# Second cross attention of a perceiver block: queries once, then turned to context space

## The reference, cut to what matters

```
q = layernorm(x) @ Wq            # 256 -> 16 heads x 128
k, v = ctx @ Wk, ctx @ Wv        # 128 -> 16 heads x 128
q = q * rsqrt(mean(q*q) + eps) * gq
k = k * rsqrt(mean(k*k) + eps) * gk
x = x + softmax(q @ k.T * scale) @ v @ Wo
```

## Time and profile before

| | |
|---|---|
| median of the runs | 2654.81 us |
| the profiled execution's own time | 2667.95 us |
| its span, from first to last instruction | 2666.0 us |
| busy, share of the span | PE 95%, PEld 71%, DVE 51%, ACT 48%, POOL 29% |
| mean granted TensorE clock | 0.983 |
| bridge | about 1203 to 1269 us |
| second cross attention | about 1270 to 1930 us |
| DMA, mean | 73 GB/s |

### The profile page before, as it was taken

One profiled execution on the slowest core, in us unless ns is written; L12 is line 12 of the kernel. 1 busy time (PEld: TensorE's weight loads), 2 busy tenths in 40 slices (PEclk: granted clock), 3 DMA queues, 4 the chain that ended last, 5 costly groups with the idle time before them and its releaser, 6 DMA issues. The chain is left out here.

```text
span 2666.0 us, 56230 instructions
## 1 busy us (share of the span) xinstructions
PE 2538.4 (95%) x16582; PEld 1904.6 (71%) x16582; DVE 1350.9 (51%) x4801; ACT 1269.6 (48%) x5190; POOL 769.3 (29%) x979
## 2 busy tenths in 40 slices
PE   7999999999999999998899999999879999999888
PEld 6888888878544444445677777777768888888777
DVE  3555555546677754446434455444424444444434
ACT  2555555544466666665545665556412222222142
POOL 1332232347355520003424323231061111111132
PEclk9999999999899999999999999999989999999999
DMA  6222222110510024422534543333380000000033
GB/s 191 71 63 65 66 64 66 53 46 0 167 48 2 1 72 134 128 58 62 145 103 125 138 111 93 85 100 89 107 205 5 8 8 8 5 7 8 8 92 122
DMA packets 176273, 195.16 MB, mean 73 GB/s; under 512 B 39993, under 2 KB 141687, under 8 KB 175378
## 3 DMA queue, kind: packets, MB, share of 16 engines
q1 hardware_dynamic: 146146, 157.65, 20.6%
q0 software_dynamic: 17744, 32.60, 5.3%
q10 hardware_dynamic: 12256, 3.44, 0.8%
HBM read 150.44 MB, written 56.62 MB: 78 GB/s over the span
## 5 line engine op out<-in xcount | busy, mean ns | idle before, releaser
L2326 PE MATMUL sa_work_ps<-sa_xnT,all_big 128*128 128x128 f32 x2048 | 243.0, 281 | 18.1 <-POOL all_big L2661 6.6
L2326 PEld LDWEIGHTS sa_work_ps<-sa_xnT,all_big 128*128 128x128 f32 x2048 | 237.7, 196 | 22.2 <-POOL all_big L2661 6.9
L267 PE MATMUL rt_kn_key_ps<-moe_w_wk,all_big 128*128 128x512 f32 x560 | 250.4, 600 | 0.8 <-DVE moe_kn_stats L316 0.4
L755 ACT ACTIVATE xa_probsT<-xa_probsT_ps 128x256 f32<-128x256 f32 x512 | 190.9, 374 | 98.0 <-PE xa_probsT_ps L620 91.5
L600 PE MATMUL xa_misc_ps<-xa_xnT,cross_folded 128*128 128x256 f32 x1024 | 233.4, 382 | 0.7 <-ACT xa_xnT L721 0.7
L643 PE MATMUL xa_misc_ps<-cross_folded,xa_mixT 128*128 128x256 f32 x1024 | 229.3, 379 | 0.0
L600 PEld LDWEIGHTS xa_misc_ps<-xa_xnT,cross_folded 128*128 128x128 f32 x1024 | 196.4, 192 | 31.7 <-ACT xa_misc_ps L730 3.3
L2419 ACT ACTIVATE sa_kT<-sa_work_ps,sa_bias_k 128x128 f32<-128x128 f32 x256 | 73.0, 368 | 302.9 <-PE sa_work_ps L2326 302.9
L643 PEld LDWEIGHTS xa_misc_ps<-cross_folded,xa_mixT 128*128 128x128 f32 x1024 | 194.6, 190 | 26.5
L620 PE MATMUL xa_probsT_ps<-all_ident,xa_probs 128*128 128x128 f32 x1024 | 198.0, 275 | 4.7 <-DVE xa_probs L881 3.9
L747 ACT ACTIVATE xa_probs<-xa_probs,xa_shift,xa_row_scale 128x257 f32<-128x257 f32 x256 | 152.6, 596 | 89.9 <-DVE xa_shift L865 89.8
(11 more groups left out here) (395 smaller groups left out, 5025.8 us busy)
## 6 DMA issues: line engine op xcount, KB each, us to landing
all_big<-rk SPq DMA_DIRECT2D x256, 128.5 KB
xa_pair<-pairs SPq DMA_DIRECT2D x64, 256.5 KB, 14.8
pairs<-all_big SPq DMA_DIRECT2D x64, 128.5 KB, 3.1
moe_w_wk<-in_ctx_dram SPq DMA_DIRECT2D x64, 128.0 KB, 2.5
pairs<-xa_keys SPq DMA_DIRECT2D x64, 128.0 KB, 2.1
cross_folded<-in_L_ffn_w_gate_dram SPq DMA_DIRECT2D x32, 192.0 KB, 2.6
cross_folded<-in_L_ffn_w_up_dram SPq DMA_DIRECT2D x32, 192.0 KB, 2.7
ff_rows<-pairs SPq DMA_DIRECT2D x35, 128.0 KB, 2.1
```

What stands on the lines that cost most here:

```text
L267: pe.matmul(self.key_ps[m % self.banks][0:n, :], self.ctxT[:, c * P:c * P + n], self.wk[:, q * 512:(q + 1) * 512], start=True, stop=True). ...
L755: act.activation(probsT[:, b % 2, :, r * P:(r + 1) * P], probsT_ps[s % 2][:, 0:KB * P].rearrange("p (k n) -> p k n", k=KB), ACT.Copy).then ...
L2326: ins = pe.matmul(ps[:, j, :], w[:, c, h * HD:(h + 1) * HD], xnT[:, c, :], start=(c == 0), stop=(c == NC - 1))
```

## The change

Queries are computed once. Of each pair of heads `plain_queries` makes Wq.T x (4 products of 256 columns; DVE copies them to SBUF, ACT squares the copy), `turn_queries` multiplies each head by its Wk, times the gains, into context space (2 products of 256 columns, kept by ACT), and `sum_squares` sums the squares of four heads by 4 products with a matrix of ones that is 32 columns wide, each into its own 32 partitions. DVE transposes the sums, POOL makes `row_scale` in 4 portions. In `bridge` the transposes of Wq and the two products of 128 columns go; `folded` holds Wk.T times the gains and, as before, Wv Wo. On SP the wait on `n_made` becomes one on `plain_made`. The core of the diff:

```diff
-            sp.wait_ge(n_made, ITERS * (G * NQ))
+            sp.wait_ge(plain_made, ITERS * HP)
...
+            def plain_queries(g, hp):
+                if hp >= 2:
+                    pe.wait_ge(plain_kept, g * HP + hp - 1)
+                for j in range(2):
+                    h = 2 * hp + j
                     for c in range(NC):
+                        ins = pe.matmul(misc_ps[hp % 2][:, j * N:(j + 1) * N], wq[:, c, h * HD:(h + 1) * HD], xnT[:, c, :],
+                                        start=(c == 0), stop=(c == NC - 1))
+                ins.then_inc(plain_made, 1)
+            def turn_queries(g, hp):
+                pe.wait_ge(plain_kept, g * HP + hp + 1)
...
+                for j in range(2):
+                    ins = pe.matmul(score_ps[hp % 2][:, j * N:(j + 1) * N], folded[:, 2 * hp + j, 0:P], plain[:, hp % 2, j, :], ...)
+                ins.then_inc(q_made, 1)
+            def sum_squares(g, r):
+                pe.wait_ge(plain_squared, g * HP + 2 * r + 2)
...
+                for j in range(HR):
+                    pe.matmul(probsT_ps[r % 2][j * T:(j + 1) * T, r // 2 * N:(r // 2 + 1) * N], ones[:, :], squares[...],
+                              start=True, stop=True).then_inc(summed, 1)
+            def all_queries(g, behind):
+                plain_queries(g, 0)
+                for hp in range(HP):
+                    if hp + 1 < HP:
+                        plain_queries(g, hp + 1)
+                    turn_queries(g, hp)
+                    if hp % 2:
+                        sum_squares(g, hp // 2)
+                    behind(hp)
...
             def keep_queries(g, more=False):          # DVE
+                if layer == 1:
+                    for hp in range(HP):
+                        keep_plain(g, hp)
+                        if hp % 2 and hp > 1:
+                            flip_sums(g, hp // 2 - 1)
+                        if more:
+                            for n in range(hp * TAKES // 2, (hp + 1) * TAKES // 2):
+                                take(g, n)
+                    flip_sums(g, R - 1)
+                    return
                 for hp in range(1, HP, 2):
...
-                    if more:
-                        for n in range(hp // 2 * TAKES, (hp // 2 + 1) * TAKES):
-                            take(g, n)
...
             def weigh(i, s):
-                        dve.wait_ge(rows_ready, i + 1)
+                        dve.wait_ge(rows_ready, i * R + R)
...
+                for r in range(R):                    # POOL, row_scales
+                    pool.wait_ge(sums_flipped, g * R + r + 1)
+                    link(pool.tensor_scalar(row_scale[:, :, r], flips[:, r % 2, :, 0], LN_EPS * HD, None, ALU.add))
+                    pool.tensor_tensor(row_scale[:, :, r], row_scale[:, :, r], minus_half[:, 0:NB], ALU.pow).then_inc(rows_ready, 1)
...
-                for c in range(NC):                   # bridge, fold_head
-                    pe.matmul(prod_ps[:, c * P:(c + 1) * P], w[:, c * P:(c + 1) * P], w[:, 2 * P:3 * P], start=True, stop=True)
-                pe.matmul(prod_ps[:, 2 * P:2 * P + D], w[:, 3 * P:4 * P], wo[:, h, :], start=True, stop=True).then_inc(multiplied, 1)
+                pe.matmul(prod_ps[:, 0:D], wvT[:, h % 2], wo[:, h, :], start=True, stop=True).then_inc(multiplied, 1)
```

More of the change, by code:

```diff
@@ L436, in cross_attention @@
         else:
-            q_sum, q_rms = sc.sb("q_sum", [P, G, H]), sc.sb("q_rms", [P, G, H])
-            row_scale = sc.sb("row_scale", [P, G, BT, R])
+            plain, squares = sc.sb("plain", [P, 2, 2, N]), folded[:, :, P:2 * P]
+            flips, ones = sc.sb("flips", [P, 2, NB, T]), sc.sb("ones", [P, T])
+            row_scale = sc.sb("row_scale", [P, NB, R])
             key_scale = key_scales(ctxT)
@@ L670, in iteration, with mix_rest @@
                 pe.wait_ge(xnT_ready, i + 2)
[L671 to L674, removed]
+                def mix_rest(hp):
                     if 1 <= hp <= LAG:
                         mix(i, rest[hp - 1])
-                pe.wait_ge(q_kept_act, (i + 1) * (HP // 2) + HP // 2)
+                if layer == 1:
+                    all_queries(i + 1, mix_rest)
+                else:
+                    for hp in range(HP):
+                        queries(i + 1, hp)
+                        mix_rest(hp)
+                    pe.wait_ge(q_kept_act, (i + 1) * (HP // 2) + HP // 2)
                 project(i, 0, range(H // 2))
@@ L691, in _ @@
             if layer == 1:
[L692 to L695, removed]
+                pe.wait_ge(ones_set, 1)
+                all_queries(0, lambda hp: None)
+            else:
+                for hp in range(HP):
+                    queries(0, hp)
                 pe.wait_ge(last_loaded, 16)
@@ L722, in keep_xnT, with square, keep_turned_queries, all_queries @@
                                ).then_inc(xnT_ready, 1)
[L724 to L731, removed]
+            def square(g, hp):
+                r = hp // 2
+                act.wait_ge(plain_kept, g * HP + hp + 1)
+                if not isinstance(g, int) or r >= 2:
+                    act.wait_ge(summed, HR * (g * R + r - 1))
+                at = r % 2 * H // 2 + hp % 2 * 4
+                act.activation(squares[:, at:at + 4, :], plain[:, hp % 2, :, :].rearrange("p j (a n) -> p (j a) n", n=P),
+                               ACT.Square).then_inc(plain_squared, 1)
+            def keep_turned_queries(g, hp):
+                act.wait_ge(q_made, g * HP + hp + 1)
+                act.activation(qT[:, :, 2 * hp:2 * hp + 2, :].rearrange("p b h t -> p h b t"),
+                               score_ps[hp % 2][:, :].rearrange("p (h b t) -> p h b t", h=2, t=T), ACT.Copy).then_inc(q_kept, 1)
+            def all_queries(g, behind):
+                square(g, 0)
+                for hp in range(HP):
+                    if hp + 1 < HP:
+                        square(g, hp + 1)
+                    keep_turned_queries(g, hp)
+                    behind(hp)
             def keep_queries(g, hp):
@@ L782, in iteration, with last_mix @@
                     return
[L783 to L786, removed]
+                def last_mix(hp):
                     if hp == 4:
@@ L789, in iteration @@
                 if layer == 1:
-                    act.wait_ge(rows_ready, i + 2)
+                    all_queries(i + 1, last_mix)
+                    act.wait_ge(rows_ready, (i + 2) * R)
+                else:
+                    for hp in range(0, HP, 2):
+                        keep_queries(i + 1, hp)
+                        last_mix(hp)
                 for s in range(EXP_AHEAD):
@@ L795, in _ @@
             if layer == 1:
[L796 to L800, removed]
+                all_queries(0, lambda hp: None)
+                act.wait_ge(rows_ready, R)
+            else:
+                for hp in range(0, HP, 2):
+                    keep_queries(0, hp)
             for s in range(EXP_AHEAD):
@@ L829, in normalize, with keep_plain, flip_sums @@
                                       ALU.subtract, ALU.mult).then_inc(normed, 1)
-            def keep_queries(g, more=False):
+            def keep_plain(g, hp):
+                dve.wait_ge(plain_made, g * HP + hp + 1)
+                if not isinstance(g, int) or hp >= 2:
+                    dve.wait_ge(q_made, g * HP + hp - 1)
+                    dve.wait_ge(plain_squared, g * HP + hp - 1)
+                dve.tensor_copy(plain[:, hp % 2, :, :], misc_ps[hp % 2][:, :].rearrange("p (j n) -> p j n", j=2)).then_inc(plain_kept, 1)
+            def flip_sums(g, r):
+                dve.wait_ge(summed, HR * (g * R + r + 1))
+                if not isinstance(g, int) or r >= 2:
+                    dve.wait_ge(rows_ready, g * R + r - 1)
+                dve.transpose(flips[:, r % 2, :, :], probsT_ps[r % 2][:, r // 2 * N:(r // 2 + 1) * N].rearrange("p (b t) -> p b t", t=T)
+                              ).then_inc(sums_flipped, 1)
+            def keep_queries(g, more=False):
+                if layer == 1:
+                    for hp in range(HP):
+                        keep_plain(g, hp)
[5 more added lines that the diff above has]
+                    flip_sums(g, R - 1)
+                    return
                 for hp in range(1, HP, 2):
@@ L1009, in row_scales @@
             def row_scales(g, link):
[L1011 to L1025, removed]
+                for r in range(R):
+                    pool.wait_ge(sums_flipped, g * R + r + 1)
+                    apart(pool, pool_passed)
+                    link(pool.tensor_scalar(row_scale[:, :, r], flips[:, r % 2, :, 0], LN_EPS * HD, None, ALU.add))
+                    pool.tensor_tensor(row_scale[:, :, r], row_scale[:, :, r], minus_half[:, 0:NB], ALU.pow).then_inc(rows_ready, 1)
+                pool.wait_ge(rows_ready, (g + 1) * R)
                 apart(pool, pool_passed)
@@ L1078, in _ @@
             if layer == 1:
+                pool.memset(ones[:, :], 1.0).then_inc(ones_set, 1)
                 next_places(1)
```

50 lines of the change are left out of this document (26 added, 24 removed).

## The result

The changed kernel takes 2700.6 us (median, 2698.7 to 2703.7) against 2652.9 us for the kernel before (2649.4 to 2657.3): ratio 1.0181, 95% interval 1.0166 to 1.0196. The forecast was 2671.3 us, with a range up to 2698. The sign is right and the time 29 us too low. The profiled executions lie closer together than the medians: 2699.45 against 2667.95 us, +31.5.

The account below looks back on a forecast made before the run. PE was taken to bound the kernel (busy 2538 of 2666 us). Bridge -9.3, boundary 0 +7.25, boundaries 1 to 6 +9.9 and boundary 7 +8.6 gave +16.5 on the 2654.8 median: 2671.3 us, range 2648 to 2698.

Parts of the forecast that it names:

- Bridge: In the bridge, dropped products and transposes and half-width DVE copies save 9.3 us (bounds 6 to 11).
- Boundary 0: At boundary 0, PE's wait for gathers 7.45, clock 2.5, late row_scale about 1.0, products -3.7: +7.25 us.
- Boundaries 1 to 6: At each, products -3.7, PE's stand for gathers behind DVE's add +3.45, clock +1.9: +1.65 us, together +9.9.
- Rival A: At the boundaries, gathers arrive early enough that they do not hold DVE and PE never stands: 2629 us; chance 0.14.
- Narrow groups: In sum_squares, 8 records of narrow products run side by side: 0.7 us a group (bounds 0.43 to 1.93).
- Rival B: In sum_squares, narrow products run one after another, 1.2 us more a group: 2708 us; chance 0.08.
- The power of 8 columns: POOL's power for row_scale takes 1.7 us, near a quarter of the 5.47 us for 32 columns.
- Clock: After PE's stand, a stretch at clock 0.50 costs 1.9 us a boundary (bounds 0 and 3.4), 2.5 at boundary 0.
- rival C: At the boundaries, PE stands but the clock stays and gathers are early in their bounds: 2654 us; chance 0.12.
- Boundary 7 and the last iteration: SP's gate opens 8.6 us later, so the last iteration's loads and its end come 8.6 us later (bounds 5 to 10).
- the products: PE's query products at a boundary fall from 28.84 to 25.1 us, 3.7 less.

Follow-up runs that it names:

- the second pair: The unchanged and the changed kernel profiled once more on chip B: 2666.7 us for the unchanged one, ratio 1.0162 for the changed one.
- late adds: Changed kernel with DVE's adds of gathered rows behind only the last four copies of a boundary, four each: ratio to before 0.9989, repeated on another chip 1.0001.
- the gate moved: Kernel before the change with SP's gate and the 16 scale loads behind the fourth item of the last iteration: ratio 0.9974.
- all three mended: Changed kernel with adds behind the last four copies, 90 increments ahead of DVE's loop, SP's gate behind the last iteration's fourth item: ratio to before 0.9822.

## Why the prediction was right in sign and too low in size

Each step against PE's timelines of the first pair of profiles:

- **Bridge**: boundary 0 starts at 1262.3 instead of 1271.3, -9.0 (forecast -9.3); in the second pair it is -11.7.
- **Boundary 0**: its iteration takes 82.4 instead of 75.6 us, +6.8 (forecast +7.25), with a stand of 7.00 us (forecast 7.45).
- **Boundaries 1 to 6, the part that was priced**: 30.9 us on average from start to projection against 28.84, +2.0 each (forecast +1.65). The stand at boundary 1 is 3.91 us, those of the six are 3.1 to 4.3 (forecast 3.45, bounds 2.9 to 4.0), PE goes on 10.1 us behind the start (forecast 9.5). The gathers' last packet comes at 7.5 us, as forecast (7.7), but DVE's first add starts at 8.6, 1.1 us behind it; the forecast had no time between the two. Rival A falls: DVE does wait for the gathers. The late adds put a price on stands and clock together: 39 to 44 us of stage time, against 6 x (3.45 + 1.9) + 7.45 + 2.5 = 42 in the forecast's terms.
- **Narrow groups**: 0.57 us (forecast 0.7). Rival B falls. The power of 8 columns takes 1.71 us (mean of 32) on POOL (forecast 1.7).
- **Clock**: rival C falls. Stretches at 0.50 between 1240 and 2040 us sum to 116 us after against 41 before. With late adds and the loop moved they are 58. In boundaries 1 to 6, up to the projection, the clock is at 0.50 for 6.8, 0, 3.4, 6.8, 3.4 and 6.8 us; half of that is 2.3 us each (forecast 1.9). The stand of 3.25 us at boundary 2 brought no drop.
- **Boundary 7 and the last iteration**: gate at 22.8 us (forecast 22.4), first score at 37.5 (38.7), +8.5 us (forecast +8.6). The gate's own 22.4 less 13.9 is 8.5, not 8.6; it changes nothing.

**The step that failed** is "Boundaries 1 to 6 each: -3.7 + 3.45 + 1.9 = +1.65, together +9.9". It prices an iteration by its query part and takes the other 51 us or so as they were, a term put at nothing without a reason. From first projection to the next boundary's start they took 51.5, 53.0, 54.0, 53.1, 50.3 and 48.9 us before and 54.4, 55.7, 55.5, 55.8, 55.4 and 49.2 after, +15.2 in all, 0.3 of it in the last, which has no taken back edge in it (+16.6 in the second pair). With this the first pair closes: -9.0 + 6.8 + 6 x 2.0 + 8.5 + 15.2 is about +33.7, and the span grew by 31.7. DVE's loop had grown from 319 to 344 records by eight copies in place of four, four transposes and the waits and register operations beside them. The working counted the time of these and not the room they take. In its new place the loop does not stay loaded, each back edge fetches its head again, and DVE stands 4 to 5 us where PE waits for it. It is the place and not the length alone: 344 records moved by 90 are not fetched again, and the old 319 moved by 32 are. Whether the change moved the loop out of its good place by the 25 records in it or by other code ahead of it, no run separates. The experiments price this at 0.8 to 1.0% in four comparisons (0.9989 to 0.9900, 1.0162 to 1.0081, 1.0001 to 0.9900, 1 to 1.0085), 21 to 27 us; all but the last are across chips. The forecast's 16.5 and this make 38 to 43 us, against 47.7 in medians in the first pair and 42.3 on chip B.

The Trainium skill, page "Runtime: NRT & Kernel Launch", section "Instruction fetch mechanics", says that a taken branch whose target is not among the two pages held makes the engine fetch it before it goes on. By that rule a loop can cost a fetch at each back edge, by the pages that it lies on, and the forecast had no term for it. The trace agrees in kind: two packets within the stand behind the branch, five for each of five back edges. The packets are of 8 KB where the page speaks of blocks of 16.

The rest of the miss is the base. The forecast added its sum to the median of the runs, while both terms and rows were of an execution 15 us slower than that. The second profiled execution of the kernel before was above the others too, by less (2666.7, median of the others 2663.2), and those of the changed kernel were not. The pair of profiles says +31.5 and the medians +47.7. Part of the excess lies in the second cross attention: from boundary 0 to boundary 7 the first profile of the kernel before has 559.4 us, where its repeat has 553.0 and the one with the gate moved, which is the same up to there, 549.6. Why is open; no run here tells it.

**Where the change's own gain is.** With all three mended, the changed kernel is 1.8% faster than the one before, and 1.5% faster than the one before with its gate moved (0.9822 / 0.9974 = 0.9848, 40 us, by ratios from two chips; their two profiled executions, 2622.7 and 2655.3 us, are 33 apart, 24.7 of it in the stage). The forecast's terms for what is saved are 9.3 for the bridge and 8 x 3.7 = 29.6 for the products, 39. The products were as cheap as hoped (25.17 us a boundary against 28.84); three costs outside them, 39 to 51 us for the place of the adds (39 to 44 by stage time, 43 to 51 by ratio), 21 to 27 for the place of the loop and some 13 for the gate (20 less the 7 that it also cost before), ate them and more.

## What to carry to other kernels

When a change adds instructions to a looped engine program, count them and look at the instruction queue's packets for each iteration, before and after; a stand "for issue" behind a back edge with packets of that queue in it points to a fetch, and filler instructions at an idle place ahead of the loop can move it away, as 90 did here and 64 did not. A new wait ahead of a copy in an in-order engine should be judged by what it waits for at the new time, and a semaphore that gates a DMA queue by the moment at which its new meaning becomes true. Add a sum that is made on a profile to that profile, and give the range the distance between it and the median.

## What the hardware showed that was not expected

- The same loop of 344 records is fetched again at every back edge or not at all, by where it lies: 100 packets and stands of 4 to 5 us, or 76 packets and 0.36 us. A shift by 64 of the changed kernel did not cure it, one by 90 did, and one by 32 brought it to the kernel before. Which places are good in general is not settled by these: in the kernel before, the loop of the first cross attention has no packets between 97 and 529 us, over seven branches of DVE.
- With a shift of 64 the stand at the back edge was 5.25 us, longer than the 4.03 without it.
- An increment of a semaphore on DVE takes 93 ns, so 64 of them are 6 us where nothing hides them.
- Chips differ. The late adds took 2689.7 us on chip A and 2660.3 on chip C. Their two profiled executions are 21.8 us apart (2688.8 and 2667.0), and 21.5 of it lie between DVE's first normalize of the first self attention and boundary 0 (721.1 and 699.6 us); from boundary 0 to the end both take 1395.0 us.
